# A mixture of experts whose first shares are spread over the partitions by TensorE in place of a transfer

## The reference

```python
def _route_dense(z, k, tau):
    topi = jax.lax.top_k(z, k)[1]
    topv = jnp.take_along_axis(z, topi, axis=1)
    w = jax.nn.softmax(topv / (tau + EPS), axis=1)
    dw = jnp.zeros((N, L), z.dtype)
    return dw.at[jnp.arange(N)[:, None], topi].add(w)

def _apply_mixture(x, dw, W):
    for e in range(W.shape[0]):                 # 12 experts
        y = y + x @ W[e].T * dw[:, e:e + 1]
...
x_addr = x_flat @ P_w.T
dw1 = _route_dense(x_addr @ U1.T, K, TAU)       # K = 3 of 12 experts
dw2 = _route_dense(x_addr @ U2.T, K, TAU)
dw3 = _route_dense(x_addr @ U3.T, K, TAU)
h = _apply_mixture(x_flat, dw1, W1)             # 128 -> 512
h = jax.nn.gelu(h, approximate=False)
y = _apply_mixture(h, dw2, W2)                  # 512 -> 128
y = y + dw3 @ b2
```

## Time and profile before

| | |
|---|---|
| median of 3 runs | 1254.43 us (1253.78 to 1258.54) |
| profiled execution, device time | 1254.49 us |
| its span in the profile | 1252.7 us |
| mean granted TensorE clock | 0.883 of full speed |
| busy: TensorE, VectorE, ScalarE, GpSimd | 79%, 62%, 42%, 34% |
| TensorE's share of the chain that ended last | 51% |
| transfers over the span | 76.55 MB |

### The profile page before, as it was taken

One profiled execution on the slowest core, in us unless ns is written; L12 is line 12 of the kernel. 1 busy time (PEld: TensorE's weight loads), 2 busy tenths in 40 slices (PEclk: granted clock), 3 DMA queues, 4 the chain that ended last, 5 costly groups with the idle time before them and its releaser, 6 DMA issues.

```text
span 1252.7 us, 19990 instructions
## 1 busy us (share of the span) xinstructions
PE 990.9 (79%) x7944; PEld 677.4 (54%) x7944; DVE 776.8 (62%) x1344; ACT 526.5 (42%) x1211; POOL 430.1 (34%) x453
## 2 busy tenths in 40 slices
PE   2669788878254389999999777769879898979888
PEld 2456466565232277878787652334456644546643
DVE  6656457564757234646464669869946656956654
ACT  4635656445025121212212060016677725768642
POOL 4373524313007300000000124528934334954420
PEclk9686777979586589999999878979989999979999
DMA  3007451717113574445431220000022210012101
GB/s 103 1 1 146 84 96 36 139 41 140 26 54 160 107 120 85 100 100 98 103 76 25 80 83 0 1 0 1 1 52 52 65 67 26 1 35 53 36 17 34
DMA packets 60719, 76.55 MB, mean 61 GB/s; under 512 B 37740, under 2 KB 42232, under 8 KB 58872
## 3 DMA queue, kind: packets, MB, share of 16 engines
q1 hardware_dynamic: 60636, 75.41, 26.7%
HBM read 52.92 MB, written 1.51 MB: 43 GB/s over the span
## 4 chain that ended last, share of the span: by engine, by line
PE 51%; DVE 17%; POOL 14%; ACT 7%; issue 5%; DMA 4%; SPq 1%; POOLq 0%; DVEq 0%
PE psum L1288 7%; PE psum L1290 7%; PE psum L1289 7%; POOL rest L1540 3%; POOL rest L1530 3%; POOL rest L1536 2%; PE psum L766 2%; PE psum L1783 2%; PE psum L1776 2%; ACT rest L1474 2%; PE psum L791 2%; PE psum L1829 2%; DMA rest<-share_d 2%; POOL rest L1566 2%; DVE main L1630 1%
## 5 line engine op out<-in xcount | busy, mean ns | idle before, releaser
L427 POOL TENSOR_TENSOR kept<-kept 128x8 f32<-128x8 f32 x8 | 1.6, 204 | 370.2 <-DVE kept L388 370.2
L1474 ACT ACTIVATE rest<-psum,main 128x128 f32<-128x128 f32 x256 | 113.4, 480 | 11.5 <-POOL main L1551 8.9
L1135 ACT ACTIVATE x_high<-main 128x512 fp32r<-128x512 f32 x48 | 30.3, 633 | 199.6 <-DVE main L1209 199.6
L1288 PE MATMUL psum<-x_high,w_low 128*128 128x512 f32 x192 | 77.0, 401 | 20.0 <-DVE x_low L1214 20.0
L1566 POOL TENSOR_TENSOR rest<-rest,main 128x512 f32<-128x512 f32 x64 | 65.4, 1044 | 45.5 <-DVE main L1636 45.5
L1289 PE MATMUL psum<-x_low,w_high 128*128 128x512 f32 x192 | 76.4, 398 | 0.0
L1290 PE MATMUL psum<-x_high,w_high 128*128 128x512 f32 x192 | 76.3, 397 | 0.0
L1288 PE MATMUL psum<-hid_high,w_low 128*128 128x512 f32 x192 | 75.6, 394 | 0.7 <-DVE main L1233 0.7
L1209 DVE TENSOR_TENSOR main<-kept,rest 128x512 f32<-128x512 f32 x48 | 33.0, 690 | 68.5 <-PE psum L1290 43.9
L1289 PE MATMUL psum<-hid_low,w_high 128*128 128x512 f32 x192 | 74.8, 389 | 0.0
L1290 PE MATMUL psum<-hid_high,w_high 128*128 128x512 f32 x192 | 74.7, 389 | 0.0
(11 more groups left out here) (332 smaller groups left out, 2784.9 us busy)
## 6 DMA issues: line engine op xcount, KB each, us to landing
rest<-share_d SPq DMA_DIRECT2D x4, 3072.0 KB, 21.0
rest<-share_d SPq DMA_DIRECT2D x4, 2304.0 KB, 20.4
main<-main SPq DMA_DIRECT2D x32, 256.0 KB, 6.1
main<-k_pad SPq DMA_DIRECT2D x16, 512.0 KB, 8.1
rest<-main SPq DMA_DIRECT2D x32, 256.0 KB, 3.5
main<-w_dram SPq DMA_DIRECT2D x2, 3072.0 KB, 13.3
main<-rest SPq DMA_DIRECT2D x32, 128.0 KB, 2.3
rest<-tables_dram SPq DMA_DIRECT2D x2, 2048.0 KB, 9.2
```

The source lines that it names most:

```text
L1288: T.matmul(dst, w_small, x_large, start=first, stop=False)
L1474: last = A.activation(probs[:, p, 4 * r + m, :], bank[2 * p + r][:, m * P:(m + 1) * P], ACT.Exp, scale=row_scale[:, c, r, m:m + 1], bias=r ...
```

## The change

For block 0, the shares of experts 0 to 5 for the first router no longer come by transfer. TensorE multiplies `weightT` of the block (36 rows, 512 tokens) by a stationary operand that is one column of the identity read 128 times, so that each of the 128 output partitions holds the selected row. There are six such products, into banks 4 to 7 and then 4 and 5 again. ScalarE copies each into `share1`, and its high copies of experts 0 to 2 are placed behind copies 3, 4 and 5. VectorE's `raw(0, e)` waits for copy e. Products 4 and 5 wait for copies 0 and 1, whose banks they take.

The transfers of `share1` are now of six rows and six, with the first left out in block 0. In block 0, SP waits until the six rows have landed before it issues `share2`. SP's loop is written out, and its semaphore `turn` is gone. The semaphores of the router's steps on TensorE (`moe_addr_ps`, `moe_logit_ps`, `moe_wT_ps`) are one, `moe_route_ps`, counted in order over 16 steps by the table `ROUTED`; those renamed waits are left out below.

```diff
@@ moe_act @@
-            for e in range(AHEAD):
-                high(0, e)
+            for e in range(SPREAD):
+                act.wait_ge(sem("moe_route_ps"), ROUTED[f"share{e}"])
+                A.activation(share1[:, e, :], bank[4 + e % 4][:, :], ACT.Copy).then_inc(sem("moe_share_copied"), 1)
+                if e >= SPREAD - AHEAD:
+                    high(0, e - (SPREAD - AHEAD))
@@ moe_dve_blocks, raw(b, e) @@
-                if e in (0, AHEAD):
-                    dve.wait_ge(sem("moe_share_in1" if e else "moe_share_in0"), b * 16 + 16)
+                if isinstance(b, int) and b == 0:
+                    dve.wait_ge(sem("moe_share_copied"), e + 1)
+                elif e == 0:
+                    dve.wait_ge(sem("moe_share_in0"), b * 16)
+                elif e == SPREAD:
+                    dve.wait_ge(sem("moe_share_in1"), b * 16 + 16)
...
                 raw(0, e)
                 low(0, e - 1)
+            dve.wait_ge(sem("moe_share_copied"), SPREAD)
             with dve.Fori(0, BLOCKS - 1) as b:
@@ moe_pe @@
             pe.wait_ge(sem("moe_wT"), BLOCKS)
+            for e in range(SPREAD):
+                if e >= 4:
+                    pe.wait_ge(sem("moe_share_copied"), e - 3)
+                one_row = ident[0:ROUTERS * EXPERTS, EXPERTS + e:EXPERTS + e + 1].to_broadcast([ROUTERS * EXPERTS, P])
+                T.matmul(bank[4 + e % 4][:, :], one_row, weightT[:, 0:512], start=True, stop=True).then_inc(sem("moe_route_ps"), 1)
@@ block.sync @@
-            with sp.Fori(0, BLOCKS) as b:
-                free = sp.snap(b + 1)
-                for r, (dst, name) in enumerate(((share1, "1"), (share2, "2"))):
-                    sp.wait_ge(sem("moe_share_free" + name), free)
-                    sp.sem_inc(sem("turn"), 1)
-                    rows = share_d[(r + 1) * EXPERTS:(r + 2) * EXPERTS, bass.ts(b, 512)]
-                    if r == 0:
-
-                        sp.dma_start(dst[:, 0:AHEAD], rows[0:AHEAD].partition_broadcast(P)).then_inc(sem("moe_share_in0"), 16)
-                        sp.dma_start(dst[:, AHEAD:], rows[AHEAD:].partition_broadcast(P)).then_inc(sem("moe_share_in1"), 16)
-                    else:
-                        sp.dma_start(dst, rows.partition_broadcast(P)).then_inc(sem("moe_share_in2"), 16)
+            for b in range(BLOCKS):
+                rows1, rows2 = (share_d[r * EXPERTS:(r + 1) * EXPERTS, 512 * b:512 * b + 512] for r in (1, 2))
+                sp.wait_ge(sem("moe_share_free1"), b + 1)
+                if b:
+                    sp.dma_start(share1[:, 0:SPREAD], rows1[0:SPREAD].partition_broadcast(P)).then_inc(sem("moe_share_in0"), 16)
+                sp.dma_start(share1[:, SPREAD:], rows1[SPREAD:].partition_broadcast(P)).then_inc(sem("moe_share_in1"), 16)
+                if b == 0:
+                    sp.wait_ge(sem("moe_share_in1"), 16)
+                sp.wait_ge(sem("moe_share_free2"), b + 1)
+                sp.dma_start(share2, rows2.partition_broadcast(P)).then_inc(sem("moe_share_in2"), 16)
```

More of the change, by code:

```diff
@@ L1117, in s4_sp_layer @@
                 sp.wait_ge(sem("s4_h"), one * BLOCKS)
+        SPREAD = 6
+        ROUTED = {name: n + 1 for n, name in enumerate([f"addr{b}" for b in range(BLOCKS)] + ["logit0", "logit1"] + [f"wT{b}" for b in range(BLOCKS)]
+                                                       + [f"share{e}" for e in range(SPREAD)])}
         def moe_act(act):
@@ L1163, in moe_dve @@
             for b in range(BLOCKS):
-                dve.wait_ge(sem("moe_addr_ps"), b + 1)
+                dve.wait_ge(sem("moe_route_ps"), ROUTED[f"addr{b}"])
                 V.tensor_copy(addr[:, 512 * b:512 * b + 512], bank[b][0:ADDR, :]).then_inc(sem("moe_addr"), 1)
@@ L1167, in moe_dve @@
             for i in range(2):
-                dve.wait_ge(sem("moe_logit_ps"), i + 1)
+                dve.wait_ge(sem("moe_route_ps"), ROUTED[f"logit{i}"])
                 link(V.tensor_copy(logit[:, half * i:half * (i + 1), :],
@@ L1190, in moe_dve @@
             for b in range(BLOCKS):
-                dve.wait_ge(sem("moe_wT_ps"), b + 1)
+                dve.wait_ge(sem("moe_route_ps"), ROUTED[f"wT{b}"])
                 V.tensor_copy(weightT[:, 512 * b:512 * b + 512], bank[b][0:36, :]).then_inc(sem("moe_wT"), 1)
@@ L1271, in moe_pe @@
                 ln_out(pe, LN_B, (b,))
-                T.matmul(bank[b][0:ADDR, :], pw_sb, hT[:, 512 * b:512 * b + 512], start=True, stop=True).then_inc(sem("moe_addr_ps"), 1)
+                T.matmul(bank[b][0:ADDR, :], pw_sb, hT[:, 512 * b:512 * b + 512], start=True, stop=True).then_inc(sem("moe_route_ps"), 1)
             half = TILES // 2
@@ L1278, in moe_pe @@
                 if c % half == half - 1:
-                    last.then_inc(sem("moe_logit_ps"), 1)
+                    last.then_inc(sem("moe_route_ps"), 1)
             pe.wait_ge(sem("moe_weight"), 1)
@@ L1283, in moe_pe @@
                 if c % 4 == 3:
-                    last.then_inc(sem("moe_wT_ps"), 1)
+                    last.then_inc(sem("moe_route_ps"), 1)
             pe.wait_ge(sem("moe_wT"), BLOCKS)
+            for e in range(SPREAD):
[3 more added lines that the diff above has]
+                T.matmul(bank[4 + e % 4][:, :], one_row, weightT[:, 0:512], start=True, stop=True).then_inc(sem("moe_route_ps"), 1)
             def thrice(dst, w_large, w_small, x_large, x_small, first, last):
```

## The result

| | before | changed |
|---|---|---|
| median | 1254.20 us (6 runs, 1252.73 to 1258.54) | 1244.11 us (6 runs, 1240.74 to 1248.50) |
| profiled execution, its span | 1254.49 us, 1252.7 us | 1240.90 us, 1239.1 us |

The ratio is 0.9917 with a 95% interval of 0.989 to 0.9944: the change makes the kernel 0.8% faster, 10.1 us between the medians. The forecast was 1238.2 us, from 1235 to 1244; the median lies 0.1 us beyond the slow end of that. Lines have moved: L1209 is now L1220, L1214 is L1225, L1288 to L1290 are L1305 to L1307, L1309 is L1326. L1302 is the product that selects a row, L1154 its copy.

A forecast was written before the change was run, and what follows sets the result against it. TensorE was taken as the bound, held up by block 0's share transfers. Earlier start 5.2, hole 6.3, low clock 4.55 and latency 0.2 us made 16.3 us saved: 1238.2 us forecast, range 1235 to 1244.

The forecast's parts named there:

- The start of the copies and of raw 0: Block 0, ScalarE and VectorE: copy 0 made and first raw product (L1209) started near 417.5 us, not 425.6.
- The price of a product at the low clock: Six selection products on TensorE: 1.71 us each at the low clock, 0.86 us at the high.
- the high end for it: Loads of the products' one-column operand: up to 2.8 us if none is hidden; taken as nothing, kept for the range.
- The rise of the clock among the products: TensorE, block 0: clock rises at 419.0, 4.2 us into the products, so experts start at the high level near 422.5.
- the products don't count for the clock: Rival, chance 0.12: products stay low until 425.1, experts run low 4.9 us more; 11.4 us saved, 1243.0 us.
- The range: Whole kernel: from 1235 us, just beyond an immediate clock rise, to 1244, products not raising the clock plus some unhidden loads.
- The second hole: TensorE's 6.29 us standstill before 442.16, block 0: closes because six transferred rows land at 430.6, 4.1 us to spare.
- share2 behind its wait, and blocks 1 to 3: Later share transfers: `share2` lands at 452 with 10 us to spare, blocks 1 to 3 stay hidden; no cost.
- The shift goes through to the end: After block 0's first phase: its 16.3 us saving carries through unchanged, span from 1252.7 to 1236.4 us.

The follow-up runs named there:

- The run over 128 rows: Changed kernel with the six products contracting over 128 rows, the added rows filled with 0.5 against a zero stationary column: median 1239.76 us, ratio 0.9875.
- three products: Changed kernel with three experts' shares made by TensorE and nine transferred (`SPREAD = 3`): median 1248.54 us, ratio 0.9959.
- the split alone: Kernel before with only its first-router share transfers cut six and six in place of three and nine: median 1250.74 us, ratio 0.9984.
- The three versions with wide products: Changed kernel with products over 128 rows: alone (ratio 0.9875), with 24 dummy matmuls ahead (0.9864), with 20 dummies and earlier products and high copy (0.9846).
- the one with dummies: Changed kernel, products still over 36 rows, plus 24 unread 128-row matmuls on TensorE ahead of the shares' transposes: median 1246.73 us, ratio 0.9938.
- the last version: Changed kernel with 20 dummy matmuls, products over 128 rows starting after the first `weightT` copy, first high copy behind copy 1: median 1234.30 us, ratio 0.9846.

## Why the prediction was nearly right, and where it failed

Point by point:

- **The start of the copies and of raw 0: right.** Raw 0 was forecast 2.8 us after the last copy and came 2.8 us after it. The copies took 0.60 us each.
- **The price of a product at the low clock: right.** ScalarE's copies of them follow each other every 1.71 us, as forecast; all six products take 10.6 us. No load of the one-column operand shows as a gap on TensorE: the high end for it, 2.8 us, did not come. That end was itself priced too low, from the load of a 64-column operand: a load took 0.33 us here, and 12 of them would be 4.0 us.
- **The rise of the clock among the products: this is the step that failed.** I had it 4.2 us after the first product, from L1272 and the two restarts. It did not come in any of the four profiles of the changed kernel. The products took 10.6 us in place of 7.3, so the experts started 10.6 us after the last copy in place of 7.8, and then ran low for 3.4 us, which costs 1.7. That makes 4.5 us: the stage was forecast at 41.1 us (to the bias matmul, 0.4 us behind the last expert) and took 45.5. This is the rival "the products don't count for the clock", with 11.4 us of saving; the stage shows 11.9 (and 11.0 to 11.9 over all pairs of profiles), since the experts ran low for 3.4 us where the rival had 4.9. The run over 128 rows is the counterproof: the rise came, and its stage took 41.6 us, within 0.5 us of the forecast. Every stream that I took the rise from contracted over 128 rows, and I argued from the duration of L1309 that 36 rows cost the same. They do in time per matmul; for the clock they don't in any of these runs, and the duration of a row could not tell that. The rival had been given 0.12. The trace of the kernel before held a hint that the prediction passed over: eight float32 matmuls over 32 rows (L652) start at 92.98 with the clock at 1.00, and from 95.0 to 98.2 it is 0.50, with TensorE busy throughout. It had been idle for 2.5 us ahead of them, so that row alone would not have settled it.
- **The range: it nearly held by the rival's price.** The forecast's own path missed by 5.9 us. The slow end of the range stood at 1244 because it counted the rival and part of the loads. The rival's condition came, the loads cost nothing, and the median still lies 1.1 us beyond the rival's 1243.0, through the other parts. That the measured time is so near the range is in part luck.
- **The second hole: right.** It is gone; the six rows landed 10.9 us after issue, with 11.8 forecast, and three products or the split alone moved it as the theory says (50.4 and 52.6 us of stage, with 51.4 and 53.6 expected).
- **share2 behind its wait, and blocks 1 to 3: right.** The rest of the experts takes 239.2 us in place of 239.3.
- **The shift goes through to the end: only in part.** The profiled span fell by 13.6 us, 11.9 of it in the stage and the rest in parts that the change does not touch. But the medians fell by 10.1 us and, on another chip, by 7.4, where the stage gave 11 to 12 in every profile. The parts around it vary by up to 8.6 us between two executions of the changed kernel. The forecast had no term for that.

What stays open: whether the changed kernel meets the longer executions more often than the kernel before, and why. In this case the parts around the stage sum to 1200.3 and 1200.9 us in two of the five profiles of the changed kernel (the four above and the one without SP's wait, 1200.3), and to 1195.3 and 1195.9 in the two of before. The three versions with wide products lost nothing of what their stage gained (stage 15.8, 18.1 and 18.8 us less than before, median 15.2, 19.9 and 19.2 less). Of those with narrow products, the one with dummies had a stage 15.4 and 12.1 us shorter in its two profiles and a median only 8.2 us lower. The split alone, with no product at all, gained 4.8 us of stage and 2.7 of median, which is within what the medians can tell. No run shows a reason.

## What to carry to other kernels

A product on TensorE can take the place of a store and a broadcast load when it is the latency that is on the path: here 10.6 us against 13 us for the start, and 11 to 12 us with the hole that the transfers had kept open. Look which operation of an in-order queue stands ahead of work that is ready: raw 3 holding back low 2 had cost 6.3 us of hole and 2.1 us for the restart at the low clock, of the 11.9 us gained. And where a narrow contraction stands alone on TensorE for many us, read the granted clock under it. Padding it to all rows cost one fill of 0.49 us on VectorE, off the path, and took 3.9 us off the stage; the last edits of its order took 0.7 us.

## What the runs showed of the hardware

- **A busy TensorE does not have to raise the clock.** The 12 records of products over 36 rows kept TensorE busy for 10.5 us at 0.50; over 128 rows the clock rose 4.9 us after the first; and with the clock up beforehand it fell to 0.50 under the narrow products, in one profile 4.0 us after their start at 412.5, in the other within 1.7 us of 416.33. Under the same products over 128 rows it stayed at 1.00. The Trainium skill, page "TensorE: Matmul & The Clock Gate", section "Part 1: The HAM clock gate", has it that sustained activity releases the clock and that this goes by time. By that rule as I read it the products would have raised the clock; they did not, and the measurement decides.
- **VectorE's raw product took 1.84 us in place of 0.69 while GpSimd was subtracting.** In the changed kernel the row of L1220 has a maximum of 1837 ns with a median of 691, and GpSimd's subtractions of the second weights end at 418.2, after the first raw product began at 416.9:

```profile
413.29 4.92 POOL L2006 TENSOR_TENSOR w_low<-main,w_high 128x512 fp32r<-128x512 f32 x4
```

VectorE's copy of `weightT` at 413.45, which reads PSUM alone, took 0.68 us beside them as it does everywhere. In the last version GpSimd runs until 422.5, and both raw and low operations there take up to 1.77 and 1.75 us. The kernel before did not show it, because its first raw product came at 425.6, after GpSimd had ended at 418.8. The Trainium skill, page "SBUF — State Buffer", section "Terms", says that VectorE and GpSimd take turns at one pair of ports for a whole instruction, and that the loser is blocked; the numbers fit that, also in the run with three products, where GpSimd ends at 419.2: the raw product that began at 417.96 took 1.84 us and the one at 420.98 took 0.69. No run here takes GpSimd's work away to prove it.
